# Moving keys and values, layer-1 attention pieces and expert lists in the first phase of a four-layer transformer kernel

## What is computed

```python
x = x + L0_xattn(layernorm(x), ctx)     # 16 heads of 16, softmax over 128 keys with a distance bias
x = x + L0_ffn(layernorm(x))            # router in pairs, 8 small experts and a shared one
x = x + L1_xattn(layernorm(x), ctx)     # per row: 16 "heads" attend causally to the 16 head slices of the same row's context
x = x + L1_ffn(layernorm(x))            # 8 experts, 2 a row, hidden 512
x = x + L2_xattn(...); x = x + L2_ffn(...)
x = x + L3_xattn(...); x = x + L3_ffn(...)   # 8 experts, 2 a row, hidden 1024
```

## Time and profile before

| | |
|---|---|
| median of 3 runs | 1716.42 us (1716.3 to 1718.08) |
| profiled execution | 1716.88 us, its span 1715.1 us |
| TensorE, VectorE, ScalarE, GpSimd busy | 1327.7, 832.6, 433.3, 287.6 us |
| first phase, from group 0's end to `router0` | 112.05 to 476.58 us of the span |
| first load of rows for L1's experts turned on TensorE | 620.41 us |

### The profile page before, as it was taken

The page is one execution under the profiler, slowest core; times in us unless marked ns, Lnnn a source line. Parts: engine busy times, 40 slices in busy tenths (PEclk is TensorE's granted clock), DMA queues, the critical chain, the costliest instruction groups (busy, mean ns, idle before and its releaser), DMA issues. The chain is left out here.

```text
span 1715.1 us, 26091 instructions
## 1 busy us (share of the span) xinstructions
PE 1327.7 (77%) x8177; PEld 1078.8 (63%) x8189; DVE 832.6 (49%) x2298; ACT 433.3 (25%) x1098; POOL 287.6 (17%) x306
## 2 busy tenths in 40 slices
PE   5877587685636248998988786877439999999997
PEld 3554444453423147888875565655329999999996
DVE  2258868778778731221233848485632222222222
ACT  2635245244112001111132232322101111111111
POOL 2010030020100020000023435351421111111111
PEclk9786686588777579999988898888759999999999
DMA  9992010010192258888820011100047888888884
GB/s 343 346 289 61 1 62 0 0 61 0 39 310 95 98 203 290 289 296 297 293 67 25 17 33 38 37 26 13 25 180 278 318 315 314 313 317 313 313 315 165
DMA packets 116307, 291.38 MB, mean 170 GB/s; under 512 B 8192, under 2 KB 90528, under 8 KB 101024
## 3 DMA queue, kind: packets, MB, share of 16 engines
q1 hardware_dynamic: 106032, 273.00, 45.5%
q0 software_dynamic: 10224, 17.77, 4.1%
HBM read 218.84 MB, written 71.90 MB: 170 GB/s over the span
## 5 line engine op out<-in xcount | busy, mean ns | idle before, releaser
L725 PE MATMUL bank<-norm_cols,work 128*128 128x128 f32 x3744 | 461.8, 277 | 20.8 <-DMA work<-in_moe 19.6
L725 PEld LDWEIGHTS bank<-norm_cols,work 128*128 128x128 f32 x3744 | 449.0, 193 | 38.8 <-issue 21.5
L1536 DVE TENSOR_TENSOR extra<-bank,span 128x256 f32<-128x256 f32 x234 | 99.2, 425 | 465.1 <-ACT span L1343 465.1
L725 PE MATMUL bank<-work,extra 128*128 128x256 f32 x936 | 240.0, 380 | 0.0
L1343 ACT ACTIVATE span<-bank 128x256 f32<-128x256 f32 x234 | 89.9, 384 | 541.9 <-PE bank L725 523.4
L725 PEld LDWEIGHTS bank<-work,extra 128*128 128x128 f32 x936 | 160.4, 191 | 12.5
L2634 POOL DMA_INDIRECT out_x<-att_rows,slot_token x39 | 60.7, 1556 | 378.0 <-ACT att_rows L1353 313.6
L2455 POOL TENSOR_TENSOR rstd<-var_eps,neg_half 128x4 f32<-128x4 f32 x17 | 17.3, 1018 | 501.6 <-DVE var_eps L1548 501.6
L725 PE MATMUL bank<-weights,norm_cols 128*128 128x512 f32 (+1 forms) x192 | 89.2, 614 | 12.2 <-ACT norm_cols L1374 5.5
L725 PE MATMUL bank<-work 128*128 128x256 f32 (+4 forms) x260 | 70.7, 418 | 28.0 <-ACT work L1374 12.7
L1280 ACT ACTIVATE work<-bank,row_max 128x128 f32<-128x128 f32 x256 | 69.8, 392 | 41.2 <-DVE row_max L1598 41.1
(11 more groups left out here) (330 smaller groups left out, 1965.6 us busy)
## 6 DMA issues: line engine op xcount, KB each, us to landing
work<-in_moe SPq DMA_DIRECT2D x78, 1024.0 KB, 7.5
work<-in_moe SPq DMA_DIRECT2D x39, 2048.0 KB, 7.8
work<-in_moe SPq DMA_DIRECT2D x39, 512.0 KB, 6.1
expert_rows_in<-zero SPq DMA_DIRECT2D x3, 5590.0 KB, 47.1
expert_rows_in<-zero SPq DMA_DIRECT2D x3, 5504.0 KB, 36.0
expert_rows_out<-zero SPq DMA_DIRECT2D x3, 5504.0 KB, 33.7
att_cols<-expert_rows_in SPq DMA_DIRECT2D x39, 130.0 KB, 2.0
att_cols<-expert_rows_in SPq DMA_DIRECT2D x39, 128.0 KB, 3.3
```

Of the source, the lines that this page charges most:

```text
L725: return pe.matmul(o, l, r, start=a, stop=z)
L1536: return dve.tensor_tensor(o, a, b, op)
```

## The change

Four things, and what follows from them:

- **Keys and values of the next group** (`keys_values`) stand behind the output projection of a group, on TensorE and ScalarE, instead of at the next group's head.
- **Layer 1's attention**: nine pieces ahead of the first maxima, "shifted" behind unit 6; none between the attention and the second norm. The value pieces that remain go between the steps of the FFN, `until("end")` behind its last add. The first norm of the next group is taken within the FFN.
- **Lists**: those of group g - 2 are made in the attention of group g (`listed`), in portions by LIST_STEPS; `xT3`, `lg1` and `rk` are in the attention's steps. Group 2's lists are made in `routed_start` and the first turn of `routed`.
- The hardware loop is gone: four copies in a row. SP loads CG2 and CG2D (context rows of layer 1) with a semaphore each; GpSimd's scatter and `x_bias` are moved behind the second norm's power.

```diff
+LIST_RING = {**UNIT_RING, "xT3": PROB_RING, "lg1": PROB_RING, "rk": SCORE_RING}
...
-L1_FRONT, L1_STEP, L1_SHIFT = 10, 4, 5
+L1_FRONT, L1_STEP = 9, 4
+SHIFT_AT = 6
+LIST_STEPS = [0, 0, 0, 0, 3, 6, 1, 4]
+TURN_AT, LOGITS_AT, EXP_AT, PAIR_AT, RANKS_AT = 1, 3, 5, 9, 9
...
+    def att_steps(lists):
+
+        order = []
+        for n in range(UNITS + 4):
+            order += [(a, n - lag) for a, lag in (("s", 0), ("p", 2), ("v", 3)) if 0 <= n - lag < UNITS]
+            if n >= 5 and n % 2 == 1:
+                order.append(("o", (n - 5) // 2))
+            if lists:
+                order += [(a, 0) for a, at in (("xT3", TURN_AT), ("lg1", LOGITS_AT), ("rk", RANKS_AT)) if n == at]
+        return order
...
+        keys += [("aT", 0), ("aT", 1)] + [("xo", t) for t in range(T)]
+        keys += kv_keys if more else []
+        keys += [("xT1", 0), ("xT1", 1)]
...
+    jk = bp.phase(kv_keys, 1)
+    j1 = [bp.phase(keys1(g >= 2, g < GROUPS - 1), 1, None, (), LIST_RING) for g in range(GROUPS)]
+    jv = [jk] + j1[:GROUPS - 1]
+    jr0 = bp.phase(l1_keys[0:3] + [("cnt",), ("gt",)] + l1_keys[3:], 1)
...
+                for g in range(1, GROUPS):
+                    sp.wait_ge(sem("shifted16"), g)
+                    load_ctx2(CG2, ctx_in, g, "ctx2_loaded")
+                    if g + 2 < GROUPS:
+                        next_ctx1(g + 2)
+                    if g >= 2:
+                        rows_gone(g - 1)
                     sp.wait_ge(sem("normed_l1"), g)
-                    load_ctx2(ds(g * T, T))
-                    sp.wait_ge(sem("rows_sent"), 16 * 2 * T * g)
...
+                    load_ctx2(CG2D, ins["ctx_by_dim"], g, "ctx2_by_dim_loaded")
+                rows_gone(GROUPS - 1)
...
-            def phase1(plan, turn, g, prev):
+            def keys_values(plan, g):
+
                 pe.wait_ge(sem("ctx_loaded"), 16 * (g + 1))
...
+            def phase1(g, listed):
+                plan, kv, turn = j1[g], jv[g], 0
                 pe.wait_ge(sem("normed"), 2 * g + 1)
...
-                for a, i in att_order:
+                for a, i in att_steps(listed is not None):
                     t, j, u, w = i // 2, i % 2, i % KB, i % SB
-                    if a == "s":
+                    if a == "xT3":
+                        layer1_turned(plan, turn, listed)
+                    elif a == "lg1":
+                        layer1_logits(plan, turn)
+                    elif a == "rk":
+                        list_ranks(plan, turn, listed)
+                    elif a == "s":
...
                 rows1(plan, turn, "xo", W0["o"], aT)
-                if prev is not None:
-                    layer1_logits(plan, turn, prev)
+                if g < GROUPS - 1:
+                    keys_values(plan, g + 1)
                 pe.wait_ge(sem("normed"), 2 * g + 2)
...
                     if s == "up":
-                        if i == 2 and prev is not None:
-                            list_ranks(plan, turn, prev)
                         ps, b = fill(plan, turn, ("up", i))
...
             def routed_start():
+                layer1_turned(jr0, 0, GROUPS - 2)
+                layer1_logits(jr0, 0)
                 pe.wait_ge(sem("choices_counted"), 1)
...
                 last.then_inc(bank_full[b], 1)
+                list_ranks(jr0, 0, GROUPS - 2)
                 ready(jr0, 0, ("gt",))
...
+            keys_values(jk, 0)
+            for g in range(GROUPS):
+                phase1(g, g - 2 if g >= 2 else None)
             routed_start()
...
+                    if listed is not None and n == EXP_AT:
+                        router_exp(listed)
+                    if listed is not None and n == PAIR_AT:
+                        pair_exp(listed)
...
-                    if n == L1_SHIFT and prev is not None:
-                        exps16(prev + 1)
+                    if g > 0 and n == SHIFT_AT:
+                        exps16(g)
+                    if listed is not None and n == TURN_AT:
+                        copy_cols(plan, turn, "xT3", kT)
                 copy_cols(plan, turn, "aT", aT)
-                if prev is not None:
-                    copy_cols(plan, turn, "xT3", kT)
+                if g < GROUPS - 1:
+                    keys_values(plan)
                 copy_cols(plan, turn, "xT1", xT)
-                if prev is not None:
-                    router_exps(prev)
...
+            copy_cols(jr0, 0, "xT3", kT)
             router0_exp()
+            router_exps(GROUPS - 2)
             for g in range(GROUPS):
...
+            def first_stats(g):
+                norm_stats(lambda t: xg(g, t), 1e-5)
+
+            def first_rows(g):
+                norm_apply(lambda t: xg(g, t), lambda t: XN[:, t, :], 2 * g + 1, "normed")
+
+            def phase1(g, listed):
+                plan, turn = j1[g], 0
+                prev = g - 1
+                left = Pieces([] if g == 0 else layer1_pieces(prev, 2 * prev + 1, prev + 1) + layer1_rows_out(prev, 2 * prev + 2))
                 some, until = left.some, left.until
+                weights = Pieces([] if listed is None else [lambda: logits_out(plan, turn)] + list_weights(plan, turn, listed, listed, True)).some
+                places = Pieces([] if listed is None else list_places(plan, turn, listed, listed, True)).some
...
-                    if n == L1_SHIFT:
+                    if n == SHIFT_AT:
                         until("shifted")
+                    weights(LIST_STEPS[n])
                     if n >= 6 and n % 2 == 0:
                         norm_out((n - 6) // 2)
                 some(L1_STEP)
                 norm_out(T - 3)
                 some(L1_STEP)
                 norm_out(T - 2)
-                some(L1_STEP)
+                places(3)
                 norm_out(T - 1)
-                until("end")
+                places(6)
                 dve.wait_ge(sem("x_biased"), g + 1)
                 for t in range(T):
                     ps, b = full(plan, turn, ("xo", t))
@@ -1629,10 +1685,7 @@
                     evacuated(plan, turn, ("xo", t))
                 alone()
                 norm(lambda t: xg(g, t), lambda t: XN[:, t, :], 1e-5, 2 * g + 2, "normed")
-
-                if prev is not None:
-                    logits_out(plan, turn)
-                    lists(plan, turn, prev, prev, True)
+                some(4)
                 dve.wait_ge(sem("x_loaded"), 16 * (GROUPS - 1))
 
...
                        SG0[:, b, :].rearrange("p (a n) -> p a n", a=2), ALU.mult).then_inc(bank_empty[b], 1)
+                    some(2)
+                    if i == 1 and g < GROUPS - 1:
+                        first_stats(g + 1)
+                    if i == 2 and g < GROUPS - 1:
+                        first_rows(g + 1)
                     if i > 1:
                         add_y(i - 2)
+                        some(2)
                 add_y(T - 2)
+                some(1)
                 add_y(T - 1)
                 for t in reversed(range(T)):
                     evacuated(plan, turn, ("acc", "y", t))
+                until("end")
                 settle()
...
-                some(4)
+                weights(14)
+                some(1)
...
                 def inverse():
+                    dve.wait_ge(sem("ctx2_by_dim_loaded"), 16 * (g + 1))
                     settle()
...
+            for group in range(GROUPS):
+                straight(lambda: phase1(group, group - 2 if group >= 2 else None))
             def last_rows():
 
                 last = GROUPS - 1
                 late = Pieces(layer1_pieces(last, 2 * last + 1, GROUPS, LATE))
-                routed_start(late.some)
+                former = GROUPS - 2
+                weights = Pieces([lambda: logits_out(jr0, 0)] + list_weights(jr0, 0, former, former, True)).some
+                places = Pieces(list_places(jr0, 0, former, former, True)).some
+                routed_start(late.some, weights)
                 for g in range(GROUPS):
                     routed_pairs(g)
+                    if g == 0:
+                        places(9)
...
+            def phase1(g, sent):
+                prev = g - 1
+                if g > 0:
                     power(2 * prev + 1, "_l1")
-                    if sent is not None:
-                        scatter(sent, NA)
-                x_bias(g)
-                if prev is not None:
+                power(2 * g + 2)
+                if sent == 0:
+                    pool.wait_ge(sem("lists_zeroed"), 16 * zrows.shape[0])
+                if sent is not None:
+                    scatter(sent, NA)
+                if g < GROUPS - 1:
+                    power(2 * g + 3)
+                    x_bias(g + 1)
+                if g > 0:
                     power(2 * prev + 2, "_l1")
-                power(2 * g + 2)
 
             def layer1(g):
-                for n in range(3):
-                    power(2 * g + (n + 1), "_l1")
+                power(2 * g + 1, "_l1")
+                scatter(g - 1, NA)
```

(42 more changed lines are left out.)

113 lines of the change are left out of this document (39 added, 74 removed).

## The result

| | before | after |
|---|---|---|
| median, same chip | 1714.58 us | 1723.16 us |
| ratio (18 runs each) | | 1.0062, 95% interval 1.0046 to 1.0079 |
| profiled execution, its span | 1716.88, 1715.1 us | 1721.93, 1720.2 us |
| VectorE busy, its instructions | 832.6 us | 828.4 us, 2298 |
| `router0` at | 476.58 us | 477.64 us |

The kernel is slower by 0.62%, clear of the 0.2% that can be told. The time lies in front of the experts: their first rows are turned 8.7 us later, the medians differ by 8.6.

What follows compares the result with a forecast made beforehand. VectorE was taken to bound the first phase, TensorE the experts. First-phase terms summed to 360.4 us against 364.5, 4.1 less; with 9.4 added behind `router0`, 1716.88 became 1722.2, stated as 1722.0 us; range 1704 to 1733.

Steps and rivals of the forecast that it cites:

- front of group 1: From group 0's last add to group 1's first maxima: 10.2 us instead of 18.2, without keys, values and first norm.
- attention of groups 1, 2, 3: From a group's first maxima to its last `norm_out`: 53.7 us, and 63.6 each with list work and two new waits.
- The waits for bank 4: Groups 2 and 3, ahead of the maxima of units 4 and 5: 2.6 and 3.0 us, ends 0 and 5.2 each.
- Group 0: Keys and values behind its output projection make `xT1` late; with part covered, the group was put 2.8 us later.
- The rest of group 2: From its last `norm_out` to its last add: 39.8 us, one more than group 1 for a projection at low clock.
- The rival of the high clock: TensorE stays at the high clock in projections and attention chains: 22 us less over three groups, 1700; chance 0.15.
- projections at the high clock as a sign that it is wrong: Output projections behind attention were expected mostly at low clock; running at the high clock would show the forecast wrong.
- The low-clock rival for keys and values: Keys and values behind the projection run at 1.2 GHz, 16 to 17 us for 9.0: some 13 more, 1735; chance 0.10.
- GpSimd beside VectorE: `x_bias` and `scatter` beside VectorE's FFN work slow it by 1.0 us a group, ends 0 and 2.4.
- the term of 2.7 for the copies: ScalarE's copies of `xT3` ahead of `router0`'s exponential: 2.7 us added, a 1.97 us TensorE turn plus 0.7 for copies.
- The list work: Group 2's lists, new in `routed_start` behind `router0`: 10.5 us less a wait of 3.52 and 0.3 covered, 6.7 added.
- The 5.3 us at `router0`: VectorE's wait of 5.26 us at `router0` goes with the loop; the rival that it stays, 1727.5, had chance 0.08.

Runs made afterwards that it cites:

- Experiments 1 and 2: After, the logits copied out ahead of unit 4's maxima: ratio to before 1.0024; after, the logits' product behind unit 4's scores, copied out behind its maxima: 0.9988.
- experiment 4: After, with keys and values of a group at its head again, all else unchanged: ratio to before 1.0104.
- experiment 3: After, with ScalarE's exponential for `router0` placed ahead of the copies of `xT3`: ratio to before 1.0058.
- before again: The kernel before, unchanged, as a run of its own against before: ratio 1.0017.
- experiments 3 and 9: experiment 3, and after with nine value pieces instead of four between the second norm and the first gate product: the latter's ratio to before 0.9970.
- experiment 11: After, logits' product behind unit 4's scores, nine value pieces before the gate, `router0`'s exponential before `xT3` copies, first division directly behind unit 6's maxima: 1674.65 us, ratio to before 0.9811.

## Why the prediction was right, and where its terms were off

It forecast 1722.0 us, slower, and 1723.16 came. The mechanism that it named came too: two waits around `lg1` in groups 2 and 3 and none in group 1, and work added behind `router0`. The shares were not as forecast. By its sum the first phase would be 4.1 us shorter in spite of the waits, and the 9.4 us behind `router0` would make the kernel slower. Measured, the first phase was 1.1 us longer (365.6 for 364.5) and the part behind it 7.7. Its sum for the first phase, term by term against the first profile of after (365.6 us where it had 360.4):

| | predicted | measured |
|---|---|---|
| group 0, later by | 2.8 | 0.8 |
| front of group 1 | 10.2 | 9.8 |
| attention of groups 1, 2, 3 | 53.7, 63.6, 63.6 | 56.4, 66.2, 68.4 |
| rest of groups 1, 2; group 3 to `router0` | 38.8, 39.8, 44.3 | 38.7, 36.2, 45.4 |
| fronts of groups 2, 3 | 21.8, 21.8 | 21.9, 21.9 |
| behind `router0`, added | 9.4 | 7.7 |

- **The waits for bank 4**: 5.6 us a group were taken, half way between the ends 0 and 10.4; units 4 and 5 waited 8.0 and 10.2 us (0.44 of unit 3's in group 3 included). Experiments 1 and 2 show that the place of `lg1` and of its copy is the cause. The term was too small, and it had no share for the product's own 1.95 and 3.58 us, which stand in unit 4's wait beside the bank's 1.91 and 1.12. The upper end, two full waits like that of unit 7, was nearer than the middle in group 3 and as far off in group 2.
- **A lost term.** Attention was summed up to the *start* of unit 7's maxima (37.6) and the tail from their *end* (16.1): 1.2 us of these maxima fell between the two in each of three groups, 3.6 in all. With them group 1 would have been 54.9. The check against group 2 of before was made at the start only and could not find it.
- **Group 0** was put 2.8 us later, for keys and values behind its projection. It ended 0.8 later, and runs with the same code for it end up to 1.5 us apart. From its last `norm_out` to its last add it took 28.7 us in after, 28.2 and 28.9 in the two profiles of before and 28.9 with keys and values at the head (experiment 4): no run shows a cost of this term.
- **Waits in group 1** of 2.31 us ahead of unit 6 and 0.40 ahead of unit 4 were not foreseen. Ahead of unit 6 TensorE first waits 1.95 us for a copy of ScalarE's (L1330); the scores then take 2.04 us, most of it at 1.2 GHz, for 1.13 a unit earlier.
- **The rest of group 2** was put one us higher, for a projection at the low clock. It ran at 3.69 us in groups 2 and 3, against 6.71 and 5.29. The rival of the high clock was right there alone, and the prediction had named projections at the high clock as a sign that it is wrong: in two groups of three that sign came, worth 3.0 and 1.6 us against before. The low-clock rival for keys and values was wrong: 1.04 a turn.
- **GpSimd beside VectorE**: 1.0 a group was taken; one product took 2.64 for 1.22 in groups 1 and 2, so 1.4. The Trainium skill ("SBUF — State Buffer", on engine access) says that the two engines hold their shared port exclusively, so that the later one stands still. The product's row agrees: it began 0.78 us after `x_bias` and ended 1.08 us behind its end. The prediction took the rule to cost `x_bias`'s whole length, 2.4 a group; it cost what was left of it when the product came. A reduction that ran beside `x_bias` from 209.57 on took its usual 0.68.
- **Behind `router0`**: the term of 2.7 for the copies measured 2.8 (the wait 3.79, 1.01 before), and experiment 3 took it away. The list work was put at 6.7 and cost 4.9 by the first two profiles, where it filled waits of 0.99 and 1.22 us that VectorE had there, and 6.5 by the second two.
- **The 5.3 us at `router0`** were taken as a gain. They were gone in after, but 3.7 of them were gone in before again too, so this was no gain of the change: the base was a slow sample by so much. No run shows what the 6.80 us of ScalarE were. The Trainium skill ("Runtime: NRT & Kernel Launch", "Instruction fetch mechanics") says that a taken branch out of the fetched window stalls an engine; no run here speaks for or against that as their cause.

The errors had both signs: some 10 us too little in the attention, some 7 too much elsewhere. That the total came within 2 us is luck in part. The forecast of the difference, 5.3 us, was low in both comparisons, which have 8.6 and 14.1 by the medians: by the waits, and by the stall that it counted as won.

## What to carry to other kernels

A small product that borrows a bank of a tight ring can cost two waits for its bank besides its own 2 to 3.6 us (8.0 and 9.8 us a group here in units 4 and 5): put it behind the work that the bound engine waits for, and empty its bank at once. The engine that bounds a stage still has stretches of 4 to 5 us of idle time in which movable pieces lie for nothing; count the pieces left behind the last step and move as many there. A stall without a releaser in one profile is looked for in a second one before it enters a sum.

## What was not expected

- The projection behind the attention ran at 3.69 us, for 5.2 to 6.7 before, in groups 2 and 3 in both profiles of after. In these groups `rk`'s small products lie in the attention's last steps, but that does not explain it: the projection took 3.69 in group 1 without them in experiments 3 and 9, 5.46 in group 3 with them in experiment 4, and 6.15 in group 2 with them in experiment 11. The cause stays open.
- Sixteen products of 8 columns each took 1.95 us at the high clock and 3.58 at the low one.
- One product on VectorE took 2.64 us for 1.22 beside GpSimd's work, with the rows around it unchanged.
- Group 0, whose code is the same in all these runs but experiment 4 and the versions of before, ended between 112.89 and 114.41 us. A difference of 1.5 us between two single profiles tells nothing here.
